# Loading the inputs of an early-fusion block in stages: image in three pieces, text in four, late constants behind them

## What is computed

```python
h = einsum('bsk,ek->bse', patches(x), w) + b     # 36 patches of 768 values per image, to 128 features
h = concatenate([h, txt], axis=1)                # 36 + 512 = 548 positions per batch, 16 batches
h = h + L0_attn(layernorm(h), W1, b1, W2, b2, gamma, beta, norm_scale)
h = h + L0_ffn(layernorm(h), ...)                # 32 experts, top-k tokens per expert
h = h + L1_attn(layernorm(h), ...)               # spiking attention
h = h + L1_ffn(layernorm(h), ...)                # shared and routed experts
# L0_attn norms once more itself: x * rsqrt(mean(x^2) + 1e-6) * norm_scale
```

## Time and profile before

| | us |
|---|---|
| runs: median (lowest to highest) of 3 | 1698.32 (1694.06 to 1701.26) |
| the profiled execution, time | 1694.06 |
| its span in the trace | 1692.3 |
| first matmul of the embedding | 12.51 |
| first matmul of the norm | 27.12 |
| first DMA issue of the gated attention | 94.56 |

### The profile page before, as it was taken

One profiled execution on the slowest core, in us unless ns is written; L12 is line 12 of the kernel. 1 busy time (PEld: TensorE's weight loads), 2 busy tenths in 40 slices (PEclk: granted clock), 3 DMA queues, 4 the chain that ended last, 5 costly groups with the idle time before them and its releaser, 6 DMA issues. The chain is left out here.

```text
span 1692.3 us, 27305 instructions
## 1 busy us (share of the span) xinstructions
PE 1313.1 (78%) x8747; PEld 922.6 (55%) x8747; DVE 1006.4 (59%) x1912; ACT 786.4 (46%) x1420; POOL 869.9 (51%) x880
## 2 busy tenths in 40 slices
PE   5679999999984431487662784888889888999997
PEld 3567777777752320376552563333333357877775
DVE  2765555555537776221111488888888566667886
ACT  3224444444443421232220345787877567664443
POOL 1454445444431004488886532777677045745766
PEclk9889999999996556699996687999999999999999
DMA  5061000000001012444444400000000121233443
GB/s 176 1 246 72 0 0 0 0 0 0 0 0 27 0 38 70 91 94 80 84 84 99 139 1 2 2 2 0 0 0 1 65 96 51 91 100 46 53 62 40
DMA packets 84440, 80.92 MB, mean 48 GB/s; under 512 B 18266, under 2 KB 73016, under 8 KB 82960
## 3 DMA queue, kind: packets, MB, share of 16 engines
q1 hardware_dynamic: 56163, 59.44, 11.0%
q0 software_dynamic: 26176, 19.40, 8.3%
q10 hardware_dynamic: 2016, 1.00, 0.2%
HBM read 46.23 MB, written 39.64 MB: 51 GB/s over the span
## 5 line engine op out<-in xcount | busy, mean ns | idle before, releaser
L1953 PE MATMUL at_slot<-at_qm,at_ks 128*128 128x512 bf16 (+1 forms) x640 | 160.4, 384 | 19.4 <-DVE at_clip L2158 10.2
L2822 POOL DMA_INDIRECT out_h<-ff_tokens x70 | 109.0, 1558 | 74.6 <-DVE ff_tokens L2875 56.0
L509 PE MATMUL ga_kv<-ga_kern,ga_v 128*128 128x274 f32 x512 | 133.5, 403 | 13.5 <-ACT ga_kern L598 12.6
L2037 ACT ACTIVATE at_clip<-at_slot,at_four 128x1024 bf16<-128x1024 f32 (+1 forms) x96 | 106.8, 1113 | 32.1 <-PE at_slot L1953 30.3
L1436 POOL DMA_INDIRECT moe_sums<-ex_y,slot_sums x69 | 108.4, 1571 | 22.2 <-issue 21.3
L2158 DVE TENSOR_SCALAR at_clip<-at_slot 128x1024 bf16<-128x1024 f32 (+1 forms) x96 | 116.1, 1217 | 3.0 <-PE at_slot L1953 2.7
L660 POOL TENSOR_TENSOR ga_rot<-ga_by_cos,ga_by_sin 128x274 f32<-128x274 f32 x64 | 48.6, 759 | 134.8 <-DVE ga_by_sin L704 134.8
L509 PEld LDWEIGHTS ga_kv<-ga_kern,ga_v 128*128 128x128 f32 x512 | 92.2, 189 | 37.8 <-ACT ga_kern L598 16.8
L2812 POOL DMA_INDIRECT by_group<-mx_stage,mx_place_i x69 | 72.2, 1046 | 48.7 <-ACT mx_stage L2698 27.9
L1526 DVE TENSOR_SCALAR ex_share<-ex_rows,owner_sb 128x1 f32<-128x1 f32 x31 | 6.6, 214 | 147.6 <-PE ex_ps_y L1478 147.6
L590 ACT ACTIVATE ga_rot<-ga_rot 128x274 f32<-128x274 f32 x128 | 53.4, 429 | 84.6 <-POOL ga_rot L660 75.2
(11 more groups left out here) (481 smaller groups left out, 3881.2 us busy)
## 6 DMA issues: line engine op xcount, KB each, us to landing
moe_sums<-ga_zeros SPq DMA_DIRECT2D x8, 1152.0 KB, 13.4
ar_rows<-moe_sums SPq DMA_DIRECT2D x34, 256.0 KB, 3.8
ex_down<-in_down SPq DMA_DIRECT2D x32, 192.0 KB, 2.6
by_group<-in_blank SPq DMA_DIRECT2D x1, 4655.0 KB, 19.9
ff_tokens<-by_group SPq DMA_DIRECT2D x17, 266.0 KB, 3.1
token_rows<-ct_rows SPq DMA_DIRECT2D x17, 256.0 KB, 2.4
out_h<-mx_rows SPq DMA_DIRECT2D x22, 192.0 KB, 2.1
H<-in_text SPq DMA_DIRECT2D x1, 4096.0 KB, 21.4
```

The source lines that it names most:

```text
L509: last = nc.tensor.matmul(kv[:, e, 0:HALF], v[p][:, mt + 2 * side, e * P:(e + 1) * P], kern[(p + g) % 2][:, side, :], start=mt == 0 and si ...
L1953: last = nc.tensor.matmul(to[r0:r0 + r, g % 2, :].rearrange("p (s n) -> p s n", s=2), ks[m][:, t * P:t * P + r], qm[m][:, 2 * g:2 * g + 2, ...
L2037: nc.scalar.activation(to[0:r], of[0:r], ACT.Relu, bias=four[0:r], scale=-1.0).then_inc(by_act, 1)
L2822: nc.gpsimd.indirect_dma_start(out=out, out_offset=bass.IndirectOffsetOnAxis(ap=ids, axis=0), in_=R[j % RING], in_offset=None, bounds_chec ...
```

## The change

SP now issues the image and its weights in three pieces of two slabs, each piece with a semaphore of its own, then the three writes of `bias_parts`, then the text in four pieces, one for each set of the norm, each with its own semaphore, and then nine of the 14 constants (`LATE_CONSTS`). ACT's queue keeps five constants. SP's only wait at the end of the block is for `bias_parts` to have landed. The six single rows are read back at the start of the next block, and SP waits there for them and for the late constants. PE runs the slabs outermost, with a wait ahead of each piece, and the norm's PE stream waits for the text of set i before it centres set i. ACT does one activation on a single column (`warm`) ahead of the embedding's.

```diff
@@ layernorm @@
+        @block.sync
+        def _(sp):
+            for part in range(3):
+                r = slice(32 * part, 32 * part + 1)
+                sp.dma_start(k["down_b3"][r, :], k["bias_parts"][part:part + 1, 0:NE, :].rearrange("o e d -> o (e d)")).then_inc(k["late_in"], 16)
+                sp.dma_start(k["b1_v3"][r, :], k["bias_parts"][part:part + 1, NE:BIAS_ROWS, :].rearrange("o e d -> o (e d)")).then_inc(k["late_in"], 16)
+            sp.wait_ge(k["late_in"], 16 * (len(LATE_CONSTS) + 6))
...
                 c = 8 * i + n
+                if n == 0:
+                    pe.wait_ge(k["text_in"][i], 16)
...
+LATE_CONSTS = ("W1", "W2", "same_expert", "earlier_group", "router", "group_row", "lanes", "owner", "odd")
@@ load_inputs @@
-                  ("ident", "ident"), ("W1", "W1"), ("W2", "W2"), ("same_expert", "same_expert"),
-                  ("earlier_group", "earlier_group"), ("router", "router"), ("group_row", "group_row"), ("lanes", "lanes"),
-                  ("owner", "owner"), ("odd", "odd")]
+                  ("ident", "ident")]
+        H4 = H[:, 0:NT].rearrange("p (g i s) -> p i g s", g=NGRP, i=NGRP)
...
             sp.dma_start(bias_rest[:], x["bias_rows"]).then_inc(bias_in, 16)
-            sp.dma_start(patches[:], x["patches"].rearrange("k p n -> p k n")).then_inc(img_in, 16)
-            sp.dma_start(tok_w[:], x["tok_w"].rearrange("k p n -> p k n")).then_inc(img_in, 16)
-            sp.dma_start(Hb[:, :, PATCHES:S], x["text"]).then_inc(text_in, 16)
-
+            for m in range(STAGES):
+                at = slice(m * TOK_K // STAGES, (m + 1) * TOK_K // STAGES)
+                sp.dma_start(patches[:, at], x["patches"][at].rearrange("k p n -> p k n")).then_inc(image_in[m], 16)
+                sp.dma_start(tok_w[:, at], x["tok_w"][at].rearrange("k p n -> p k n")).then_inc(image_in[m], 16)
             sp.wait_ge(cut, 6)
             for part in range(3):
                 sp.dma_start(parts_d[part], bias_part[part][:]).then_inc(laid, 16)
+            for i in range(NGRP):
+                sp.dma_start(H4[:, i, :, PATCHES:S], x["text"][:, i]).then_inc(text_in[i], 16)
+            for name in LATE_CONSTS:
+                sp.dma_start(k[name][:], x[name]).then_inc(late_in, 16)
             sp.wait_ge(laid, 48)
-            for part in range(3):
...
-            sp.wait_ge(laid, 144)
-            sp.wait_ge(img_in, 32)
-            sp.wait_ge(text_in, 16)
...
+            nc.scalar.activation(warm[:], k["cols"][:, at:at + 1], ACT.Identity, bias=k["cols"][:, at:at + 1])
...
-            pe.wait_ge(img_in, 32)
-            for j in range(2):
-                for t in range(TOK_K):
+            for t in range(TOK_K):
+                if t % (TOK_K // STAGES) == 0:
+                    pe.wait_ge(image_in[t * STAGES // TOK_K], 32)
+                for j in range(2):
                     last = nc.tensor.matmul(emb[j][:, 0:half], tok_w[:, t, :], patches[:, t, j * half:(j + 1) * half],
                                             start=t == 0, stop=t == TOK_K - 1)
-                last.then_inc(embedded, 1)
+                    if t == TOK_K - 1:
+                        last.then_inc(embedded, 1)
@@ _arrays @@
-    a["text"] = np.asarray(inp["txt"]).transpose(2, 0, 1)
+    a["text"] = np.asarray(inp["txt"]).transpose(2, 0, 1).reshape(P, NGRP, NGRP, TEXT).transpose(0, 2, 1, 3)
```

More of the change, by code:

```diff
@@ L267, in load_inputs @@
         emb = [st.enter_context(nc.psum_tensor(f"embedding{j}", [P, 512], F32)) for j in range(2)]
-        parts_d = nc.dram_tensor("bias_parts", [3, BIAS_ROWS, P], BF16, kind="Internal").ap()
         bias_rest = st.enter_context(nc.sbuf_tensor("bias_rest", [BIAS_ROWS, P], F32))
         bias_part = [st.enter_context(nc.sbuf_tensor(f"bias_part{n}", [BIAS_ROWS, P], BF16)) for n in range(3)]
-        img_in, text_in, const_in, embedded, evacuated, bias_in, cut, laid = (
-            sem(n) for n in ("image", "text", "const", "embedded", "evacuated", "bias", "cut", "laid"))
+        const_in, embedded, evacuated, bias_in, cut, laid = (sem(n) for n in ("const", "embedded", "evacuated", "bias", "cut", "laid"))
+        STAGES = 3
+        image_in = [sem(f"image{m}") for m in range(STAGES)]
+        late_in, text_in = k["late_in"], k["text_in"]
+        warm = st.enter_context(nc.sbuf_tensor("warm", [P, 1], F32))
+        parts_d = k["bias_parts"]
         half = B * PATCHES // 2
@@ L290, in _ @@
                 sp.dma_start(parts_d[part], bias_part[part][:]).then_inc(laid, 16)
+            for i in range(NGRP):
+                sp.dma_start(H4[:, i, :, PATCHES:S], x["text"][:, i]).then_inc(text_in[i], 16)
+            for name in LATE_CONSTS:
+                sp.dma_start(k[name][:], x[name]).then_inc(late_in, 16)
             sp.wait_ge(laid, 48)
-            for part in range(3):
-                r = slice(32 * part, 32 * part + 1)
-                sp.dma_start(k["down_b3"][r, :], parts_d[part:part + 1, 0:NE, :].rearrange("o e d -> o (e d)")).then_inc(laid, 16)
-                sp.dma_start(k["b1_v3"][r, :], parts_d[part:part + 1, NE:BIAS_ROWS, :].rearrange("o e d -> o (e d)")).then_inc(laid, 16)
-            sp.wait_ge(laid, 144)
-            sp.wait_ge(img_in, 32)
-            sp.wait_ge(text_in, 16)
         @block.scalar
@@ L340, in _ @@
                 nc.vector.tensor_copy(k["pick_wide"][32 * g:32 * g + 32, g], k["pick_row"][32 * g:32 * g + 32])
-    nc.clear_and_free_semaphores([img_in, text_in, const_in, embedded, evacuated, bias_in, cut, laid])
+    nc.clear_and_free_semaphores([*image_in, const_in, embedded, evacuated, bias_in, cut, laid])
 def gated_attention(nc, k, x, H, HN, moe_d):
@@ L2990, in build @@
              "owner": sb("owner_sb", [P, 2, NE - 1]), "odd": sb("odd_sb", [P, TILES])}
+        k["text_in"] = [ctx.enter_context(nc.semaphore(f"text_in{i}")) for i in range(NGRP)]
+        k["late_in"] = ctx.enter_context(nc.semaphore("late_in"))
+        k["bias_parts"] = nc.dram_tensor("bias_parts", [3, BIAS_ROWS, P], BF16, kind="Internal").ap()
         k["ln2_sems"] = {n: ctx.enter_context(nc.semaphore(f"ln2_{n}")) for n in LN2_SEMS}
```

## The result

The changed kernel takes 1688.89 us (median of 4 runs, 1687.94 to 1690.34) against 1697.88 us (4 runs, 1694.06 to 1701.26): ratio 0.9948, interval 0.9926 to 0.9971. Forecast were 1689.3 and a gain of 9.0 us; measured is 9.0.

The account below looks back on a forecast made before the run. SP, held at its issues by its full queue, was taken to end the first block. An earlier norm start (8.3 us) plus the clock (0.7) made 9.0 off the 1698.3 median: 1689.3 us, range 1682.5 to 1696.0.

Parts of the forecast that it names:

- What bounds the first block: Block ahead of the norm: SP, its issues held behind the text, ends it; the norm's first matmul stands at 27.12.
- Piece by piece: Embedding with the image in three pieces: PE starts at 6.0 instead of 12.51, done at 15.0; ACT done at 16.1.
- What SP has to issue: First block's end: the last late constant gets through 8.7 us after 9.5; norm starts at 18.8, saving 8.3 us.
- The waits for the text: Norm's PE stream: each text piece lands before its set needs it, so the new waits hold nothing.
- The clock: Norm's first centring: PE idles 3.8 us instead of 5.6, so a clock kept more often gives 0.7 us.
- One for one behind the norm: Everything behind the norm starts behind its barrier and moves with it by the same time.
- a sign of being wrong: Whole kernel: forecast is wrong if the gated attention starts 9 us earlier and the end doesn't follow.
- SP not held: Rival, first block: all SP issues pass as they come, norm starts at 16.7, gain 12.6 us, 1685.7; chance 0.20.
- The queue takes less: Rival, SP's queue: only 64 rows per engine count, norm starts at 22.6, saving 4.5, time 1693.5; chance 0.15.
- Every piece pays its latency: Rival, SP's DMAs: seven more pieces hold the queue 2.1 us each, norm at 33.5, 1704.7, slower; chance 0.05.
- The row that the prediction set against it: Profile row: eight queued DMAs of 1152 KB moved at 406 GB/s over 20.6 us, so no gap each.

Follow-up runs that it names:

- late_behind: Changed kernel with its nine late constants issued from SP behind the barrier, at the head of the norm's block: 1682.5 us, ratio 0.9929 to the kernel before.
- late_first: Changed kernel with the nine late constants issued ahead of the four text pieces, all still in the first block: 1684.84 us in its one profiled run.
- after_third: The changed kernel unaltered, run a third time in the third set: 1775.04 us against 1784.09 for the kernel before, ratio 0.9948.

## Why the prediction was right

**What bounds the first block.** Right: SP, by the issues that its full queue holds back. `late_behind` takes away only what is queued, and the block ends 4.6 us earlier.

**Piece by piece.** PE started at 6.88, not 6.0 (6.55 and 6.13 in the repeats), and finished at 14.50, not 15.0: the clock rose some 3 us into the embedding (6 matmuls in 8 to 10 us, 10 in 10 to 12, by the windows shown below), while in the kernel before ten matmuls filled the first 4.83 us. Neither mattered. ACT was done at 15.04, a microsecond before the forecast: the two halves are moved in 0.99 us, back to back.

**What SP has to issue.** The term was 8.7 us from the text's start and came to 9.4: I took 110 places less 81, so 29 text rows per engine left; there were 20. Counting the DMA's own places in explains at most three of these nine rows: with the 98 to 102 that the trace of before shows ahead, 26 to 30 rows would be left. The rest is that the last constant was taken with 92 ahead, the low end of what the six cases show. So the term rested on a count that is good to some ten places, 0.9 us; the 20 rows lie just outside the 21 to 39 that the prediction allowed. 108 rows at the 372 GB/s of the earlier trace rows are 9.5 us, so the rate and the start at 9.5 were right. With 0.5 for the barrier instead of 0.57, the norm started 0.6 late.

**The waits for the text** held nothing, as said; the norm's matmul waited for the barrier (PEq), not for `text_in`. It would be the next bound: `late_first` ran into it.

**The clock** gave 0.67 us where I took 0.7, if the whole difference of the norms, 67.44 and 66.77 us, is put down to it. PEclk in the first centring was 0.64 against 0.60, and the first reciprocal came 0.4 us sooner behind the first matmul (8.73 against 9.12), so 0.3 us lie in later sets. Another execution of the same kernel (`after_third`) had a norm of 68.1 us, so this agreement is chance; the term is good to about 1 us either way. My reason, an idle time shorter by a third, isn't borne out: in `after_third` PE was idle for 4.37 us, the shortest of the three executions, and the first reciprocal came 9.5 us behind the first matmul, the latest.

**One for one behind the norm.** True to 627 us in the first pair (8.2 us of the 8.4 are still there), beyond that only within the scatter. So the mechanism was right and the last digit is luck. The gain agrees with the forecast to 0.1 us, better than any of its parts deserves: the start gave 8.4 and not 9.0, the rest scatters by 3 us and more, and the same two kernels differed by only 4.8 us in the second set. The prediction named as a sign of being wrong that the gated attention starts 9 us earlier and the end doesn't follow; the first pair of profiles (8.4, then 4.8) and the second set come near it, the medians of the other two don't.

**The rivals.** *SP not held* fell with the 18.90 and became real, with its price, in `late_behind`: foretold was a gain of 12.6 us with a norm at 16.7, came a norm at 14.8 and 15.8 and gains of 12.9 and 15.0. *The queue takes less* (64 places) fell. *Every piece pays its latency* fell: one DMA in place of four landed at most some 0.2 us earlier, and GB/s has no hole between the pieces of after (windows view, the last column):

```profile
8.00:10.00 2.00, 2.00 (x6) 1.43 (x5) 1.21 (x6) 0.29 (x1) 0.00 (x0) 1.00 1.07 362
10.00:12.00 2.00, 2.00 (x10) 1.58 (x9) 0.82 (x3) 0.00 (x0) 0.00 (x0) 1.00 1.06 387
12.00:14.00 2.00, 2.00 (x10) 1.58 (x9) 0.00 (x0) 0.00 (x0) 0.00 (x0) 1.00 1.04 386
14.00:16.00 2.00, 0.50 (x3) 0.04 (x1) 0.00 (x0) 0.99 (x2) 0.00 (x0) 1.00 1.05 386
```

The row that the prediction set against it was read too large: of the eight DMAs of 1152 KB, 9.4 MB, only 8.33 MB of SP's queue moved in the 20.6 us window, so seven of them at 406 GB/s. It bears the point all the same. The Trainium skill gives a DMA issued from GpSimd a fixed part of about 2 us beside its bytes ("DMA: Bandwidth & Descriptors", section "Anatomy of one DMA — SWDGE (gpsimd) path", not the section that the prediction named). Between SP's queued pieces this trace shows no such gap.

## What to carry to other kernels

A DMA issue is an instruction that can block: behind a large transfer SP's stream stood still (9.50 us at one write of 34 short rows before, 8.5 us over nine small constants after), and the end of the block then waited for the transfer, though no wait was written. So count what is issued between the last thing that is needed and the end of the block, and put transfers that nobody needs yet behind the barrier (5.9 us here, in the third set), not only behind in the queue. And before an engine is given its data earlier, see whether it then only idles: PE's earlier embedding bought 0.3 us at the barrier and let the clock fall for the first set.

## What I had not expected of the hardware

SP got through with a held issue when 91 to 102 places per engine stood in its queue ahead of that DMA, in six cases of four kernels, and it took the text's own 128 places at once behind 91. Over an idle time of PE of 0.84 or 0.86 us the clock stayed at 2.4 GHz (five profiles), over 2.09, 2.27 and 4.4 to 7.0 us it fell, which cost 1.4 to 2.7 us of the norm's first set; and the same program's norm varied by up to 2.2 us with the time spent at 1.2 GHz. In two of three sets all kernels took about 85 us more; in the profiles about 80 of them lie in the last block (298.3 us from its first DMA to the end in the first pair, 378 to 385 later) and 5.5 in the experts. The cause is open.
